# Queries of the cross-attention turned on TensorE instead of loaded already turned

## The reference

```python
scores = einsum('bqd,bkd->bqk', query, key) / sqrt(256)   # causal, padded keys to -inf
out = einsum('bqk,bkd->bqd', softmax(scores), value)
...
h = silu((x @ w1.T) * s1) * ((x @ w2.T) * s2)             # 256 -> 1024, ternary weights
h = gelu((h @ h1.T) * s3)                                 # 1024 -> 1024
h = gelu((h @ h2.T) * s4)                                 # 1024 -> 1024
out = (h @ w3.T) * s5                                     # 1024 -> 256
```

## Time and profile before

| | |
|---|---|
| runs | 372.63, 373.57, 373.64 us |
| the profiled execution's own time | 373.64 us |
| its span | 371.6 us (2.04 us lie outside) |
| PE, matmuls | 362.7 us busy, 98% |
| DVE | 178.8 us, 48% |
| ACT | 146.2 us, 39% |
| POOL | 29.3 us, 8% |
| largest group, L958 | 1024 matmuls, 400.6 us summed, as matmuls overlap |

### The profile page before, as it was taken

How to read it: one execution, slowest core, us unless ns; L and a number is a source line. 1 busy time by engine, 2 the same in 40 slices (tenths; PEclk the granted TensorE clock), 3 DMA queues, 4 the chain that set the end, 5 groups by cost and what they waited for, 6 DMA issues and landing times.

```text
span 371.6 us, 4841 instructions
## 1 busy us (share of the span) xinstructions
PE 362.7 (98%) x1773; PEld 304.6 (82%) x1773; DVE 178.8 (48%) x406; ACT 146.2 (39%) x246; POOL 29.3 (8%) x53
## 2 busy tenths in 40 slices
PE   8888999999999999999999999999999999999996
PEld 5677888888898888888889888888889888888886
DVE  3747633533565743434555763263455663232334
ACT  3668774594033632162131643134113563212120
POOL 7310040000100004000010005000010000000000
PEclk9999999999999999999999999999999999999999
DMA  7999999984331001000171000000000000000001
GB/s 252 340 362 326 320 359 262 365 337 156 126 132 60 3 3 30 0 2 4 44 212 58 4 1 22 10 2 4 0 2 31 32 3 2 2 2 2 2 2 58
DMA packets 12179, 36.52 MB, mean 98 GB/s; under 512 B 2050, under 2 KB 4996, under 8 KB 11780
## 3 DMA queue, kind: packets, MB, share of 16 engines
q1 hardware_dynamic: 11264, 35.02, 26.5%
q10 hardware_dynamic: 868, 0.80, 1.1%
HBM read 33.70 MB, written 13.64 MB: 127 GB/s over the span
## 4 chain that ended last, share of the span: by engine, by line
PE 92%; DVE 2%; issue 2%; ACT 2%; POOL 2%; POOLq 0%; DVEq 0%; ACTq 0%
PE ring L958 62%; PE ring L937 14%; PE ring L977 8%; PE att L888 2%; PE att L907 2%; PE att L878 1%; PE ring L1098 1%; DVE turned L583 1%; ACT scaled L407 1%; ACT gate L489 1%; PE att L896 1%; PE ring L1080 0%; ACT h_hi L479 0%; PE ring L1117 0%; POOL rstd L351 0%
## 5 line engine op out<-in xcount | busy, mean ns | idle before, releaser
L958 PE MATMUL ring<-h_hi,weights 128*128 128x512 f32 x512 | 201.2, 393 | 0.1
L958 PE MATMUL ring<-h_lo,weights 128*128 128x512 f32 x512 | 199.4, 390 | 0.0
L958 PEld LDWEIGHTS ring<-h_hi,weights 128*128 128x128 f32 x512 | 96.2, 188 | 20.0 <-issue 0.2
L958 PEld LDWEIGHTS ring<-h_lo,weights 128*128 128x128 f32 x512 | 96.2, 188 | 19.8
L501 ACT ACTIVATE act<-ring,scales 128x512 f32<-128x512 f32 x64 | 44.1, 689 | 156.7 <-PE ring L958 153.5
L746 DVE CAST h_hi<-act 128x512 fp32r<-128x512 f32 x64 | 27.4, 428 | 144.0 <-ACT act L501 136.0
L640 DVE TENSOR_TENSOR h_lo<-act,h_hi 128x512 fp32r<-128x512 f32 x96 | 66.6, 694 | 2.6
L937 PE MATMUL ring<-xn_hi,weights 128*128 128x512 f32 x112 | 43.7, 390 | 0.4 <-issue 0.4
L937 PE MATMUL ring<-xn_lo,weights 128*128 128x512 f32 x112 | 43.6, 390 | 0.0
L489 ACT ACTIVATE gate<-ring,scales 128x512 f32<-128x512 f32 x32 | 22.0, 689 | 36.3 <-PE ring L937 36.3
L733 DVE SCALAR_TENSOR_TENSOR act<-ring,scales,gate 128x512 f32<-128x512 f32 x32 | 24.0, 751 | 20.2 <-PE ring L937 15.8
(11 more groups left out here) (119 smaller groups left out, 240.7 us busy)
## 6 DMA issues: line engine op xcount, KB each, us to landing
weights_staged<-in_weights SPq DMA_DIRECT2D x22, 512.0 KB, 7.0
weights<-weights_staged SPq DMA_DIRECT2D x22, 512.0 KB, 5.6
x_in<-in_x SPq DMA_DIRECT2D x8, 256.0 KB, 2.9
ctx_cols<-in_ctx_cols SPq DMA_DIRECT2D x8, 256.0 KB, 4.9
ctx_rows<-in_ctx_rows SPq DMA_DIRECT2D x4, 512.0 KB, 7.1
out_dram<-residual SPq DMA_DIRECT2D x16, 128.0 KB, 2.0
turned<-in_x_cols SPq DMA_DIRECT2D x3, 512.0 KB, 7.6
mask<-in_mask SPq DMA_DIRECT2D x3, 256.0 KB
```

Of the source, the lines that this page charges most:

```text
L958: ins = nc.tensor.matmul(bank[:], w, part[:, k].bitcast(dt), start=(k == 0 and part is h_hi[src]), stop=(k == HC - 1 and part is h_lo[src]))
```

## The change

x is no longer loaded a second time, and the means make no way through HBM. Instead DVE takes the means off the rows (`normalise` with norm 0, four operations 128x256 after split 2 of layer 1, from `x_in` to `xn`, which is `work`), PE transposes the result in eight transposes 128x128 into `att` (`turn_rows` with norm 0, between chunks 4 and 5 of layer 1), and ACT copies the two banks to `turned`, scaled (`evacuate_q`, after gelu 4). `scores` waits for that copy. In tile 0's program `turn_rows` waits for the flag HID1C, and PE waits for both copies ahead of `sum_flag(HID2A)`. On SP, the second staging of pieces 0 and 1 moves from pieces 17 and 18 to pieces 9 and 10, and the values of tile 1 are loaded after piece 11 instead of 16.

```diff
-            def load_query_cols(t):
-
-                sp.dma_start(q_cols[:], x_cols_d[t].rearrange("b p c t -> p b c t")).then_inc(x_cols_in, 16)
...
-                if n in (FLAG_PIECES[LAST][0], FLAG_PIECES[LAST][0] + 1):
-                    stage(n - FLAG_PIECES[LAST][0])
+                if n in (FLAG_PIECES[HID1C][0], FLAG_PIECES[HID1C][0] + 1):
+                    stage(n - FLAG_PIECES[HID1C][0])
...
                 if n == FLAG_PIECES[HID1C][1] - 1:
-                    load_query_cols(1)
                     load_keys(1)
                     load_mask(1)
-                if n == FLAG_PIECES[HID2B][1] - 1:
                     load_values(1)
...
-                if not norm:
-                    nc.gpsimd.tensor_scalar(mean_scaled[:], mean_var[:, :, 0], SCALE, 0.0, ALU.mult, ALU.add
-                                            ).then_inc(mean_made, 1)
...
-            def store_means(t):
-
-                act.wait_ge(mean_made, t)
-                act.dma_start(means_d[t], mean_scaled[:]).then_inc(mean_stored, 16)
-
-            def spread_means(t):
-
-                act.wait_ge(mean_stored, 16 * t)
-                act.dma_start(work[:, 0:TOK], means_d[t].rearrange("p r -> (p r)").partition_broadcast(P)
-                              ).then_inc(mean_loaded, 16)
+            def evacuate_q(t):
+                for b in range(PAIR):
+                    act.wait_ge(q_turned, PAIR * (t - 1) + b + 1)
+                    nc.scalar.activation(turned[:, b * 512:(b + 1) * 512], att[b][:], ACT.Copy, scale=-SCALE
+                                         ).then_inc(q_evacuated, 1)
...
-            def centre(t, b):
-
-                dve.wait_ge(x_cols_in, 16 * t)
-                dve.wait_ge(mean_loaded, 16 * t)
-                for c in range(EC):
-                    cols = q_cols[:, b, c].rearrange("p (q t) -> p q t", q=2)
-                    nc.vector.scalar_tensor_tensor(out=cols, in0=cols, scalar=SCALE, in1=mean_cols[:, b],
-                                                   op0=ALU.mult, op1=ALU.subtract).then_inc(q_centred, 1)
-
-            def normalise(t, r):
+            def normalise(t, norm, src, r):
                 if r == 0:
-                    dve.wait_ge(moments, ROWS * 2 * t)
-                    dve.wait_ge(rstd_ready, 2 * t)
-                nc.vector.tensor_scalar(xn[:, r], x_attn[:, r], mean_var[:, r, 0:1], rstd[:, r:r + 1],
+                    dve.wait_ge(moments, ROWS * (2 * (t - 1) + norm + 1))
+                    if norm:
+                        dve.wait_ge(rstd_ready, 2 * t)
+                factor = rstd[:, r:r + 1] if norm else -1.0
+                nc.vector.tensor_scalar(xn[:, r], src[:, r], mean_var[:, r, 0:1], factor,
                                         ALU.subtract, ALU.mult).then_inc(xn_ready, 1)
...
-                        if at == (0, 6):
-                            for b in range(PAIR):
-                                centre(t + 1, b)
+                        if at == (0, 2):
+                            for r in range(ROWS):
+                                normalise(t + 1, 0, x_in, r)
...
-            def turn_rows(t):
+            def turn_rows(t, norm, done):
...
-                        pe.wait_ge(xn_ready, ROWS * (t - 1) + r + 1)
+                        pe.wait_ge(xn_ready, ROWS * (2 * (t - 1) + norm) + r + 1)
...
-                    pe.wait_ge(q_centred, PAIR * EC * (t - 1) + EC * (b + 1))
+                    pe.wait_ge(q_evacuated, PAIR * (t - 1) + b + 1)
...
                 hid1(HID1B, 4)
+                pe.wait_ge(flag_ready, HID1C + 1)
+                turn_rows(1, 0, q_turned)
                 hid1(HID1C, 5, 6)
+                pe.wait_ge(q_evacuated, PAIR)
                 sum_flag(HID2A)
...
                 hidden_segment(0, (3, 5))
+                if more:
+                    turn_rows(t + 1, 0, q_turned)
                 hidden_segment(0, (5, 8))
```

More of the change, by code:

```diff
@@ L56, with xattn_ffn @@
 FIRST_ROWS = (1, 0, 3, 2)
-def xattn_ffn(nc, x, x_cols_d, ctx_rows_d, ctx_cols_d, mask_d, weights_d, scales_d, down_scale_d, out):
+def xattn_ffn(nc, x, ctx_rows_d, ctx_cols_d, mask_d, weights_d, scales_d, down_scale_d, out):
     staged_d = nc.dram_tensor("weights_staged", [PIECES, P, PIECE], F32).ap()
-    means_d = nc.dram_tensor("means", [TILES, P, ROWS], F32).ap()
     out_v = out.rearrange("(t r p) d -> t p r d", p=P, r=ROWS)
@@ L108, in xattn_ffn @@
         inv_sum = sb("inv_sum", [P, ROWS])
-        mean_scaled = sb("mean_scaled", [P, ROWS])
         xn = work[:].rearrange("p (r d) -> p r d", r=ROWS)
@@ L123, in xattn_ffn @@
         raw_pieces = [gate[:].rearrange("p n t -> p (n t)"), residual[:].rearrange("p r d -> p (r d)")]
-        mean_cols = work[:, 0:TOK].rearrange("p (t b q) -> p b q t", b=PAIR, q=2)
         probs_t = turned[:, 0:PAIR * KEYS].rearrange("p (b k) -> p b k", b=PAIR)
@@ L142, in xattn_ffn @@
         ctx_rows_in = sem("ctx_rows_in")
[L143 to L146, removed]
         mask_loaded = sem("mask_loaded")
@@ L156, in xattn_ffn @@
         low_summed = sem("low_summed")
+        q_evacuated = sem("q_evacuated")
         probs_ready = sem("probs_ready")
@@ L177, in xattn_ffn @@
         result_done = sem("result_done")
-        q_centred = sem("q_centred")
+        q_turned = sem("q_turned")
         scores_done = sem("scores_done")
@@ L258, in load_next @@
                 load_values(t)
-                load_query_cols(t)
             def stage(n):
@@ L513, in tile @@
                             test_piece(n)
[L514 to L517, removed]
+                        if more and (layer, c) == (0, HID1_CHUNKS[1][1] - 1):
+                            evacuate_q(t + 1)
                         if more and (layer, c) == (0, HC - 1):
@@ L803, in tile @@
                             for r in range(ROWS):
-                                normalise(t + 1, r)
+                                normalise(t + 1, 1, x_attn, r)
                 if more:
@@ L878, in turn_rows @@
                             ins = nc.tensor.transpose(att[b][:, at:at + P], xn[:, r, c * P:(c + 1) * P], ident[:])
-                    ins.then_inc(xn_turned, 1)
+                    ins.then_inc(done, 1)
             def scores(t):
@@ L1041, in first_tile @@
                 hid2(LAST, 5, 6, 7)
-                turn_rows(1)
+                turn_rows(1, 1, xn_turned)
                 segment(LAST, lambda dt: down(0, dt))
@@ L1065, in tile @@
                 if more:
-                    turn_rows(t + 1)
+                    turn_rows(t + 1, 1, xn_turned)
                 segment(LAST, lambda dt: down(t, dt))
@@ L1185 @@
         "in_x": x,
-        "in_x_cols": np.asarray(inputs["x"]).reshape(TILES, PAIR, SEQ, EC, P).transpose(0, 1, 4, 3, 2),
         "in_ctx_rows": ctx.reshape(TILES, ROWS, P, EMB).transpose(0, 2, 1, 3),
```

## The result

| | before | after |
|---|---|---|
| median of 5 runs each, us | 373.57 (372.27 to 374.19) | 376.99 (375.77 to 377.52) |
| ratio, 95% interval | | 1.0096 [1.0065, 1.0126] |
| profiled execution: time, span, us | 373.64, 371.6 | 376.71, 374.6 |

The kernel became slower, as forecast, but by 3.4 us of the medians (3.1 us of the profiled executions) where I had given 2.25. The missing part is one piece.

The account below looks back on a forecast made before the run. PE, busy 98% of the span, was taken to bound the kernel. 373.64 + 2.64 (transposes) - 0.39 (wait) + 0 (loads) = 375.89 us, median 375.8; forecast's own range 375.3 to 376.6, chance 0.71.

Parts of the forecast that it names:

- The transposes: PE in tiles 1 to 3: 24 added transposes at 0.110 us each, 0.88 us a tile, +2.64 us.
- The rivals with cheap and with slow transposes: Added PE transposes: cheap at 0.057 us each, 374.5 us, chance 0.07; slow at 0.21 us, 378.3 us, chance 0.03.
- the slow one: Added PE transposes at 0.21 us each, as at the kernel's start, or slowing what follows; 378.3 us, chance 0.03.
- The wait ahead of `scores`: Tile 0's program: without `centre`, PE's wait for HID2A shrinks from 0.62 to 0.23 us, once, -0.39 us.
- DVE, ACT, the new waits: Four DVE operations, two ACT copies and PE's waits for them: hidden by 3.8 and over 8 us of cover, 0.
- The loads of tile 0: Reordered loads: pieces 12 to 16 land 3.2 us later but stay hidden; taken as 0.
- the rival of 377.2 us: Tile 0 loads slip 5 us, PE waits 1.1 us at the flag sum ahead of chunk 7; chance 0.12.
- An instruction that is added to PE costs its whole distance between starts, wherever it stands: Rule for pricing instructions added to PE's program, giving 0.110 us for each new transpose.
- the parts outside these stretches move: Sign that the prediction is wrong: times change outside the hidden stretches forecast at 67.4 us (tile 0) and 65.7 us (tiles 1, 2).

Follow-up runs that it names:

- e4: Kernel after with each of the 24 new transposes done twice; 377.98 us, ratio 1.0089 to the kernel before.
- e8: Kernel before with flag HID2A read ahead of `centre` on DVE in tile 0; 375.27 us against 374.04, ratio 0.9988.
- e7: Kernel after with the old load order and 32 never-executed TensorE instructions; 375.43 us, ratio 1.0024 to the kernel before.
- e3: Kernel before with 34 never-executed TensorE instructions in tile 1's first stretch; 375.17 us, ratio 1.0051.
- e10: Kernel after with tile 1's slow down branch and the jump over it left out; 375.25 us, ratio 1.0015 to the kernel before.
- e12: Kernel after run again, unaltered; 377.29 us, ratio 1.0091 to the kernel before.
- e5: Kernel before with 123 never-executed TensorE instructions in tile 1's first stretch; 373.77 us, ratio 1.0004.
- e9: Kernel before with 50 never-executed TensorE instructions in tile 1's first stretch; 374.90 us, ratio 1.0027.
- e1: Kernel after with 32 never-executed TensorE instructions in tile 1's first stretch; 375.84 us, ratio 1.0023 to the kernel before.
- e13: Kernel before run again, unaltered; 373.33 us in one run.
- e11: Kernel before with HID2A read ahead of `centre` and two first-token stagings issued behind the last weight load; 372.67 us against 373.61, ratio 0.9965.
- e2: Kernel after with 72 never-executed TensorE instructions in tile 1's first stretch; 375.62 us, ratio 1.0038 to the kernel before.

## Why the prediction was off

- **The transposes**, 24 at 0.110 us: 0.87 to 0.90 us a tile where 0.88 stood, confirmed by doubling them (0.87). The rivals with cheap and with slow transposes fall. The rule of the Trainium skill, "TensorE: Matmul & The Clock Gate", "Part 4: PE-mode transpose", that the full clock does not engage for transposes, stood behind the slow one; up to 16 in a row (e4) show no sign of it, at a granted clock of 1.00 and 0.11 us each. A longer row of transposes was not run.
- **The wait ahead of `scores`**, -0.39 us: 0.22 instead of 0.62 us ahead of it. `scores` itself is 0.10 us shorter too (2.44 us from its start to the next product's, where it was 2.54), which the sum did not have; so the stretch is 67.28 us and not 67.36. Both are shown alone in e8 (0.23 and 2.43).
- **DVE, ACT, the new waits**: nothing, as predicted.
- **The loads of tile 0**: no late test of piece 14, so the rival of 377.2 us fell too, although the time came out there. e7 bears out the zero.
- **What failed** is the step "An instruction that is added to PE costs its whole distance between starts, wherever it stands": the sum had no term for where the added instructions push the code behind them. The text named it as a way to be wrong: "the parts outside these stretches move". The missing term is 1.24 us at the entry into tile 2. 375.8 + 1.2 = 377.0, and 376.99 was measured; that it closes so well is luck, as the five runs spread over 1.8 us. e3, e10 and e12 show that it comes from the jump at that place; that the wait is one for code is argued.

The Trainium skill, "Runtime: NRT & Kernel Launch", section "Instruction fetch mechanics", says that instructions are prefetched in sequence in 16 KB lines, and that a taken branch whose target lies outside the two pages held stalls the engine until its page has come. The trace agrees that there are stalls at a jump (1.24 and 1.74 us). It does not say which pages were held at the jump: from every place listed above, the 259-instruction jump ends in the next block, and it is clean from most of them, in block 30 from place 18 too (e5). The same section of the Trainium skill gives TensorE's instruction memory as 128 KiB, eight such pages, so the section alone does not settle how much is held either. What I could have taken from it is a list of every long jump behind the insertion with its place, and a rival of one stall.

**Open.** Why the entry into tile 3 stays clean at places 17 and 18. In after, e12 and e3 PE goes on 2.36 to 2.38 us after the start of the last q8 transfer, and the stalls of 1.24, 1.32 and 1.74 us differ because that transfer starts 1.12, 1.06 and 0.64 us before the down product is through; why it starts later in e3 is not known. At places 34 and 50 it is another pattern: in e9, e1 and e7 PE goes on 3.64 to 3.67 us after one q8 transfer and 0.21 to 0.22 us after the start of the next. A transfer at the entry is no stall by itself: in before, e13, e8 and e11 one starts 1.05 to 1.11 us ahead of a clean entry. What in the fetch decides is therefore argued, not shown.

## What to carry to other kernels

Where an engine is busy 98% and its program has long branches that are jumped over, added instructions cost their own time plus, possibly, one fetch stall that no semaphore shows; look for "issue" idle at stage entries and move the code by some tens of never-executed instructions to tell it from work. Ask for repetition too: in tile 0 such idles of 0.2 to 0.5 us come and go between profiles with the same code there (0.48 us at 53.55 in e2, none in after). Price a term on one tile's stretch and not on the whole time, since the hidden stretches of tiles 1 and 2 repeat within 0.01 us (one exception, 0.08 in e3) where medians move by 1. Before paying for the removal of a wait early in a stage, see whether a transfer at the end of the stage decides when it ends.

## What was not expected of the hardware

- Code placement alone moved a kernel with the same executed work by 1.74 us in the profile (e3 against before).
- Behind a wait of 1.79 us TensorE's granted clock was 0.74 over the next 6.6 us (e8): the products behind it started 0.58 and then five times 0.43 us apart, the pace of the lower level, then 0.23 again. Against the kernel before this made 1.95 us up to the flag sum, 0.65 from it to the next product and 1.31 for the slow products, 3.9 us in all. The length of the wait alone does not decide: behind 1.70 us (e9) and 1.81 us (e2, at 33.26) the clock stayed at 1.00, behind 2.18 us (e11, at 33.68) it fell too. What decides was not traced. The rows are e9, e2 and e11, from the flag sum on:
```profile
87.27:93.85 6.58, 6.13 (x28) 1.00 0.03 12
33.26:39.90 6.64, 6.26 (x28) 1.00 0.88 330
33.68:39.79 6.11, 5.73 (x19) 0.72 0.91 349
```
- Run times of e8 fall into two groups some 3 us apart. That the order of the 512 KB transfers in tile 0 decides between them is argued, not shown: e11 had one run of twelve above 375.5 us, but the unaltered kernel on that chip had only five of 29. In e9 too PE waited 1.7 us for that test, though its tile 0 had begun 2.6 us earlier than before, and the stage ended at 106.14, against 106.22 before.
- The products of the start ran at half pace until about 10 us in most profiles and only until about 5 us in four (e2, e4, e9, e11), and tile 0's gate began at 18.1 to 18.3 us instead of 20.1 to 20.8. The four transposes of the earlier trace rows, 0.21 us apart, stand 0.11 us apart in those four, as in mid-stream, so the price of the slow rival was one of the slow start. The granted clock reads 1.00 in both kinds of profile. The code there is the same in all, so this varies between executions, and 2 us of it can vanish again by the end of tile 0.
